# Who applies the normalisation of the second layer's rows: VectorE or ScalarE

## What is computed

```python
def _layernorm(x, axis=-1, eps=1e-05):
    m = jnp.mean(x, axis=axis, keepdims=True)
    v = jnp.var(x, axis=axis, keepdims=True)
    return (x - m) / jnp.sqrt(v + eps)
...
    h = _layernorm(x, axis=-1) * (1 + ca) + sa
    x = x + ga * _L1_attn_ref(h, L1_attn_Wq, ...)
    h = _layernorm(x, axis=-1) * (1 + cb) + sb
    x = x + gb * _L1_ffn_ref(h, L1_ffn_router_w, ...)
```

## Time and profile before

| | us |
|---|---|
| median of 3 runs | 1859.78 (1859.64 to 1865.61) |
| the profiled execution, its own time | 1862.15 |
| its span | 1860.1 |
| busy: PE, DVE, ACT, POOL | 1661.3, 1378.9, 823.8, 692.4 |

### The profile page before, as it was taken

How to read it: one execution, slowest core, us unless ns; L and a number is a source line. 1 busy time by engine, 2 the same in 40 slices (tenths; PEclk the granted TensorE clock), 3 DMA queues, 4 the chain that set the end, 5 groups by cost and what they waited for, 6 DMA issues and landing times.

```text
span 1860.1 us, 25467 instructions
## 1 busy us (share of the span) xinstructions
PE 1661.3 (89%) x7212; PEld 1033.6 (56%) x7212; DVE 1378.9 (74%) x2632; ACT 823.8 (44%) x1540; POOL 692.4 (37%) x626
## 2 busy tenths in 40 slices
PE   2788988849889889999999999999998899999999
PEld 2355555526656556556565565665555555555555
DVE  6778777627868986988969979789699588544444
ACT  1466666637644235244243352342424543433333
POOL 2011111100001963936919639379096186000000
PEclk9999899979999999999999999999998999999999
DMA  7544444127567686666666667666663121111110
GB/s 274 160 116 132 116 117 125 48 96 208 161 195 205 193 275 188 200 188 190 198 187 195 199 185 206 179 188 203 175 196 85 37 50 53 40 51 51 54 52 24
DMA packets 167947, 269.49 MB, mean 145 GB/s; under 512 B 23220, under 2 KB 61453, under 8 KB 164661
## 3 DMA queue, kind: packets, MB, share of 16 engines
q1 hardware_dynamic: 164227, 266.40, 49.2%
q10 hardware_dynamic: 1586, 1.30, 0.2%
q0 software_dynamic: 2048, 0.79, 0.2%
HBM read 233.78 MB, written 34.62 MB: 144 GB/s over the span
## 4 chain that ended last, share of the span: by engine, by line
PE 37%; DVE 19%; issue 10%; POOL 7%; ACT 3%; DMA 2%; DVEq 0%; SPq 0%; POOLq 0%; ACTq 0%
PE psum L1361 10%; PE psum L1203 6%; PE psum L1205 6%; PE psum L1204 6%; PE psum L1214 5%; DVE psum L1803 4%; POOL e_prod L1897 4%; DVE e_hm L1806 3%; POOL e_phi L1897 3%; DVE e_state L1756 2%; DVE e_vbar L1605 2%; DVE e_y L1605 2%; PE psum L1295 1%; DMA e_ring<-w_split 1%; ACT e_gu L1537 1%
## 5 line engine op out<-in xcount | busy, mean ns | idle before, releaser
L1537 ACT ACTIVATE e_gu<-psum 128x512 f32<-128x512 f32 (+1 forms) x368 | 219.1, 598 | 569.7 <-DVE e_hm L1806 298.0
L1203 PE MATMUL psum<-e_hhi,e_ring 128*128 128x512 f32 x704 | 436.0, 619 | 26.2 <-DVE e_ring L1596 9.7
L1214 PE MATMUL psum<-e_hm,w_d 128*128 128x512 f32 (+1 forms) x736 | 385.5, 606 | 17.3 <-DVE e_hm L1806 9.7
L1897 POOL TENSOR_TENSOR e_prod<-e_state,e_phi 128x512 f32<-128x512 f32 x256 | 354.9, 1425 | 2.4 <-POOL e_phi L1897 1.7
L1803 DVE TENSOR_TENSOR psum<-psum,rw 128x512 f32<-128x512 f32 x352 | 243.7, 692 | 110.1 <-PE psum L1205 87.0
L1841 DVE TENSOR_TENSOR e_hm<-psum,rw 128x512 f32<-128x512 f32 x256 | 174.5, 688 | 176.6 <-ACT psum L1565 175.6
L1204 PE MATMUL psum<-e_hhi,e_ring 128*128 128x512 f32 x704 | 280.3, 398 | 0.0
L1205 PE MATMUL psum<-e_hlo,e_ring 128*128 128x512 f32 x704 | 280.0, 398 | 0.0
L1806 DVE TENSOR_TENSOR e_hm<-psum,e_gu 128x512 f32<-128x512 f32 x352 | 243.5, 692 | 38.9 <-ACT e_gu L1537 15.3
L1361 PE MATMUL psum<-e_hm,w_gu 128*128 128x512 f32 x512 | 262.9, 599 | 6.6 <-DVE w_d L1822 5.5
L1565 ACT ACTIVATE psum<-psum 128x512 f32<-128x512 f32 x256 | 148.8, 582 | 252.7 <-PE psum L1205 239.0
(11 more groups left out here) (262 smaller groups left out, 2201.6 us busy)
## 6 DMA issues: line engine op xcount, KB each, us to landing
e_ring<-w_split SPq DMA_DIRECT2D x308, 256.0 KB, 4.0
rw<-rw_fm SPq DMA_DIRECT2D x192, 176.0 KB
qk_parts<-at_part SPq DMA_DIRECT2D x96, 192.0 KB, 2.9
rw<-gates_fm SPq DMA_DIRECT2D x72, 256.0 KB, 3.3
w_split<-e_ring SPq DMA_DIRECT2D x44, 256.0 KB, 2.8
rw<-rw_fm SPq DMA_DIRECT2D x64, 160.0 KB
at_qs<-qk_parts SPq DMA_DIRECT2D x16, 576.0 KB
at_ks<-qk_parts SPq DMA_DIRECT2D x16, 576.0 KB
```

The costliest lines, as they stand in the source:

```text
L1203: pe.matmul(out, w_hi, x_hi, start=first, stop=False)
L1214: mm = pe.matmul(ps[:, ACC, :], weights_at(T, WD + P * j, P)[0:rows(j), :], hm[0:rows(j), slot(j), :], start=(j == 0), stop=(j == HT - 1))
L1537: a(act_g[0:r, j % 2, :], ps[0:r, GB[j % 2], :], ACT.Silu).then_inc(silu_done, 1)
L1897: ins = tt(out[:, at], x[:, at], y[:, at], op)
```

## The change

In both second-layer normalisations `dve_norm` is replaced by `dve_columns` on VectorE, in the same place, and `act_norm` on ScalarE, after the same tile (7 and 16). `dve_columns` forms the factor (reciprocal of the standard deviation) and the shift (minus mean times factor) on four columns, into two new tiles `e_minus_a` and `e_minus_b`; `act_norm` waits for them and applies them as scale and bias in four Identity activations of 128 x 128 from PSUM. TensorE's program is the same.

```diff
+        minus_a, minus_b = sb("e_minus_a", [P, CT]), sb("e_minus_b", [P, CT])
...
                     if j == 6:
                         ln_a.act_std(act, m)
+                    if j == 7:
+                        ln_a.act_norm(act, m, minus_a)
...
                     if j == 15:
                         ln_b.act_std(act, m)
+                    if j == 16:
+                        ln_b.act_norm(act, m, minus_b)
...
                     if j == 7:
-                        ln_a.dve_norm(dve, m)
+                        ln_a.dve_columns(dve, m, minus_a)
...
                     if j == 16:
-                        ln_b.dve_norm(dve, m)
+                        ln_b.dve_columns(dve, m, minus_b)
```

## The result

The changed kernel takes 1865.74 us (median of 22 runs, 1857.31 to 1871.67) and the kernel before 1859.12 us (22 runs, 1854.06 to 1869.99). The ratio is 1.0034, 95% interval 1.0021 to 1.0047: slower by 4 to 9 us, 6.6 by the medians. I had forecast 3.7 us.

What follows compares the result with a forecast made beforehand. No single engine was taken as the bound; the chain ran 37% through TensorE, 19% through VectorE. Terms 2.1 + 0 + 0.46 + 0.77 + 0 + 0.41 gave 3.7 us later, 1863.5 us, range 1857 to 1870 us.

Steps and rivals of the forecast that it cites:

- The activations stand ahead of silu 17: At b in `block0`, silu 17 queues behind the four activations on ScalarE and ends 2.67 us later than before.
- The term at b, 6 x 0.35 = 2.1 us: Six b places in `block0`: VectorE's product 17 starts 0.35 us later, passing through GpSimd to the transposes before tile 8.
- a in chunks 2 to 7, 0 us: Six a places in `block0`: silu 8 ends later but nothing needs it until 942.60; freed VectorE time only lengthens idling.
- a in chunk 1, 0.46 us: `block0`, chunk 1, where VectorE lags: silu 8 ends at 570.8, so TensorE's gate 10 starts 0.46 us later.
- `block1`, 0.77, 0 and 0.41 us: Three places in `block1`: gelus behind the activations delay up products 14, 29 and 5 by 0.77, 0 and 0.41 us.
- The sum, 3.7 us: Whole kernel: the terms at b, a and `block1` together make it 3.7 us later, factor 1.0020, 1863.5 us.
- what is removed and added: At 16 places VectorE is freed 1.2 us each, 19 in all; ScalarE gains 1.5 us each, 24 in all.
- the freed time reaches the end: Faster rival: product 17 up to 1.2 us earlier, shortening six chunks' waits before tile 8, 7.2 us, 1852.6 us; chance 0.08.
- TensorE's clock: Slower rival: 0.44 us more waiting at each b place brings lower-clock stretches, 10 us more, 1873.6 us; chance 0.12.

Runs made afterwards that it cites:

- twice: The changed kernel with the four activations at a and b in the second layer issued twice over the same rows: 1879.29 us, ratio 1.0125.
- later: The changed kernel with both sets of activations one tile later on ScalarE, behind silus 8 and 17: 1857.61 us, ratio 0.9996.
- with three increments a alone: Kernel before with the change only at a, plus three idle semaphore increments ahead of VectorE's loop (start 1538): 1859.95 us, ratio 1.0001.
- trimmed: Kernel before without eleven idle semaphore increments in VectorE's straight parts, eight put ahead of its loop (start 1538): 1858.94 us, ratio 0.9996.
- changed kernel with six increments: The changed kernel with six semaphore increments that nobody waits for ahead of VectorE's loop (start 1538): 1858.88 us, ratio 1.0003.
- relief: Kernel before with VectorE normalising only one block of four, nine idle increments keeping its loop at 1541; output differs: 1856.01 us, ratio 0.9967.
- later with six increments: Changed kernel with both activation sets one tile later on ScalarE, plus six idle increments ahead of VectorE's loop (start 1538): 1859.07 us, ratio 1.0000.
- shifted: Kernel before without eleven idle semaphore increments in VectorE's straight parts, so its loop starts at 1530: 1858.75 us, ratio 0.9998.

## Why the prediction was right in part

- **"The activations stand ahead of silu 17"**: right, and shown by twice, which pays their time a second time, and by later, where the loss is gone. ScalarE's busy time rose by 20.9 us (24 forecast), VectorE's fell by 17.3 (19), the four take 1.50 us, and no table load stands before them.
- **The term at b, 6 x 0.35 = 2.1 us**: its size is 0.30 in the loop and 0.14 to 0.15 in the two straight chunks, 1.5 us in all, read where no code is waited for. That it passes through GpSimd to the chunk's end undiminished was right. In the changed kernel itself it read 0.67, of which 0.36 is code.
- **a in chunks 2 to 7, 0 us**: right for the work: with three increments a alone has the chunk of the trimmed kernel (93.37 against 93.36) and a ratio of 1.0001. VectorE's first wait behind it grew from 1.89 to 2.97 us, as said.
- **a in chunk 1, 0.46 us**: gate 10 comes 2.53 us after the reciprocal (568.28 to 570.81), 2.03 before, so 0.50.
- **`block1`, 0.77, 0 and 0.41 us**: up product 14 at 2.54 us after the reciprocal, 1.72 before: 0.82. The third, 2.44 against 2.09: 0.35. The second came at 3.83 us instead of 2.71, in a stretch at a clock of 0.50 (0.72 before), which I put down to the clock.
- **The sum, 3.7 us**: the same terms measured give 1.5 + 0.5 + 0.8 + 0.35 = 3.1 us. The changed kernel with six increments, which has these terms and no wait for code, shows 0.5 us with an interval of 3 below to 4 above; 3.1 lies in it, and so would nothing.
- **The step that failed** is in "what is removed and added": I counted the removed instructions by their durations alone and put what their place in the program costs at nothing, without a reason. Nine instructions fewer ahead of VectorE's loop (six are enough, three are not) moved the loop's start across a border, from 1541 to 1532, and from then on VectorE waited for its own code in each round. Six idle instructions take that away, and with it 6.9 us by the medians; the time is then that of the kernel before. So most of the measured 6.6 us is a term that the forecast doesn't have, and that it came near in size is in good part luck.
- **Rival "the freed time reaches the end"**: the mechanism exists (relief, 0.9967) but silu 17 blocks it, as the forecast said. Even later with six increments wins only 0.33 us a chunk, since TensorE's transposes now wait 0.3 us longer for ScalarE and the second phi sum comes 0.37 us earlier, not 1.
- **Rival "TensorE's clock"**: not behind gate 19. The lower clock moved elsewhere, and rather less of it came: one stretch in chunks 4 to 6 where the kernel before has three. That added idle time can only cost, as I took it there, doesn't hold for the whole kernel: the added wait at the loop's start cost its own length and saved such stretches (2 in 15 against 20 in 24).

## What to carry to other kernels

An instruction moved to an engine with time to spare is paid by what is queued behind it there: put it behind the work that others wait for, not ahead of it. Compare the instruction queue's packets and the idle time marked "issue" at a loop's start before and after any edit, even one that only shortens a straight part ahead of the loop; a few idle instructions can take back what such a shift costs. And a wait that is taken away or added also moves the stretches of lower clock, so a local reading of 1 us a round can be worth nothing in the median, as between shifted and trimmed.

## What the runs showed of the hardware that I had not expected

- The instruction queue moves one or two packets of 8 KB a chunk when VectorE's loop of 334 to 340 instructions starts at 1538 or 1541 of the program as built, and seven when it starts at 1530, 1532 or 1535. The exposed wait of VectorE was 0.36 us at instruction 1664 and 0.9 to 2.0 us at the loop's start.
- Waits of TensorE of 2.2 to 2.5 us for `e_x` were followed by the lower clock in five of six rounds (0.57 over 4 us in the one shown); waits of 1.3 to 1.8 us in none of ten.
